# First weight chunk in two transfers, aligned weight rows, and six warming matmuls on a prologue constant, in a cross-attention kernel on one core

## What is computed

```
q = x @ Wq + bq;  k = ctx @ Wk + bk;  v = ctx @ Wv + bv
w = softmax(q @ k.T / sqrt(512), axis = queries)
y = w @ v + x
out = (y - mean(y)) * rsqrt(var(y) + eps) * gamma + beta
```

## Time and profile before

| | us |
|---|---|
| median of 3 runs | 142.45 |
| lowest, highest | 141.98, 142.91 |
| the profiled execution, its own time | 142.72 |
| span of the profiled execution | 141.0 |
| TensorE matmuls busy in the span | 134.5 |
| VectorE, ScalarE, GpSimd busy | 115.1, 79.6, 60.8 |

### The profile page before, as it was taken

One profiled execution on the slowest core, in us unless ns is written; L12 is line 12 of the kernel. 1 busy time (PEld: TensorE's weight loads), 2 busy tenths in 40 slices (PEclk: granted clock), 3 DMA queues, 4 the chain that ended last, 5 costly groups with the idle time before them and its releaser, 6 DMA issues.

```text
span 141.0 us, 2976 instructions
## 1 busy us (share of the span) xinstructions
PE 134.5 (95%) x1046; PEld 130.2 (92%) x1046; DVE 115.1 (82%) x224; ACT 79.6 (56%) x283; POOL 60.8 (43%) x61
## 2 busy tenths in 40 slices
PE   6999999999999999999999999999999999999940
PEld 6899999999998999999999999999999999999940
DVE  0689995996996779999999976878789976797983
ACT  4267098677276925467474829474747546386420
POOL 1000000027304580733849370629475643629791
PEclk9999999999999999999999999999999999999998
DMA  4899999965087495995988799696996965535314
GB/s 152 294 411 417 424 307 394 333 227 204 13 251 274 184 364 153 380 346 188 342 294 297 291 308 382 225 324 211 328 335 227 383 251 203 212 103 196 144 73 150
DMA packets 10814, 37.33 MB, mean 265 GB/s; under 512 B 1200, under 2 KB 1456, under 8 KB 10800
## 3 DMA queue, kind: packets, MB, share of 16 engines
q1 hardware_dynamic: 9424, 34.79, 69.6%
q10 hardware_dynamic: 1376, 2.36, 4.4%
HBM read 33.87 MB, written 3.28 MB: 263 GB/s over the span
## 4 chain that ended last, share of the span: by engine, by line
PE 89%; POOL 5%; issue 2%; ACT 1%; DVE 0%; POOLq 0%; DVEq 0%
PE ps_S L423 29%; PE ps_U L437 26%; PE ps_Y L458 10%; PE ps_U L396 6%; PE ps_Y L396 6%; POOL xT_in L978 3%; PE ps_Y L340 2%; POOL xT_in L966 2%; PE ps_S L344 1%; PE ps_w L446 1%; PE ps_U L503 1%; PE ps_U L350 1%; PE ps_c L411 1%; PE ps_U L355 1%; ACT xT_in L600 1%
## 5 line engine op out<-in xcount | busy, mean ns | idle before, releaser
L582 ACT ACTIVATE expo<-scores,negmax 121x100 f32<-121x100 f32 x96 | 35.0, 365 | 30.9 <-DVE negmax L753 30.9
L423 PE MATMUL ps_S<-G,ctxT_in 128*121 128x100 f32 (+1 forms) x384 | 43.4, 269 | 0.0
L423 PEld LDWEIGHTS ps_S<-G,ctxT_in 128*121 128x121 f32 (+1 forms) x384 | 42.1, 185 | 0.0
L437 PEld LDWEIGHTS ps_U<-prob,ctx_in 121*128 121x128 f32 x336 | 39.4, 192 | 0.9
L437 PE MATMUL ps_U<-prob,ctx_in 121*128 121x100 f32 x336 | 39.6, 274 | 0.0
L955 POOL TENSOR_TENSOR prob<-expo,rinv 121x600 f32<-121x600 f32 x16 | 19.2, 1202 | 30.6 <-DVE rinv L760 30.4
L966 POOL TENSOR_TENSOR xT_in<-x_in,xT_in 128x512 f32<-128x512 f32 (+1 forms) x13 | 17.1, 1315 | 19.8 <-issue 8.9
L749 DVE TENSOR_TENSOR scores<-ps_S,c_rows 121x600 f32<-121x600 f32 x16 | 12.5, 782 | 10.3 <-PE ps_S L423 7.4
L764 DVE TENSOR_REDUCE probsum<-prob 121x100 f32<-121x600 f32 x16 | 19.8, 1237 | 1.0 <-POOL prob L955 0.7
L582 ACT ACTIVATION_READ_ACCUMULATOR expo<-scores,negmax 121x1 f32 x96 | 17.9, 187 | 0.0
L971 POOL TENSOR_TENSOR rstd<-vareps,neg_half 128x1 f32<-128x1 f32 (+1 forms) x13 | 7.1, 549 | 23.3 <-DVE vareps L791 23.1
(11 more groups left out here) (120 smaller groups left out, 185.7 us busy)
## 6 DMA issues: line engine op xcount, KB each, us to landing
ctx_in<-ctx SPq DMA_DIRECT2D x16, 768.0 KB, 4.9
ctxT_in<-ctxT SPq DMA_DIRECT2D x16, 722.0 KB, 5.1
xT_in<-xT SPq DMA_DIRECT2D x8, 400.0 KB, 8.5
x_in<-x SPq DMA_DIRECT2D x12, 256.0 KB, 4.6
out<-xT_in ACTq DMA_DIRECT2D x8, 256.0 KB, 4.0
wqk<-Wqk SPq DMA_DIRECT2D x4, 388.0 KB, 4.6
out<-xT_in SPq DMA_DIRECT2D x3, 256.0 KB, 2.0
wv_in<-Wv SPq DMA_DIRECT2D x1, 512.0 KB, 15.7
```

The source lines that it names most:

```text
L423: last = nc.tensor.matmul(ps_scores(c)[0:rows(c), :], ctxT_in[:, q, l * M + c * MP:l * M + c * MP + rows(c)], G[:, l, bass.ds(b * T, T)], ...
L437: last = nc.tensor.matmul(ps_U[:, q, l * T:(l + 1) * T], ctx_in[0:rows(c), q, c, l * P:(l + 1) * P], prob[0:rows(c), q, c * T:(c + 1) * T] ...
L582: last = nc.scalar.activation(expo[0:MP, q, c * T:(c + 1) * T], scores[0:MP, q, c * T:(c + 1) * T], ACT.Exp, bias=negmax[0:MP, q, c:c + 1] ...
```

## The change

Four things change, all ahead of or at the first weight products.

- The chunk 0 comes in two transfers: first the columns 256 to 770 (the second half of Wq, Wk and the biases, 515 columns), with a semaphore of its own, `first_w_in`; then the columns 0 to 255, which set `w_in[0]`. The other three chunks carry 771 columns instead of 776.
- The halves swap their parts: banks 2 and 3 now get the FP32 product of chunk 0, since their columns come first; banks 0 and 1 get the split products. ScalarE's upper half of chunk 0 is that of columns 0 to 255 and waits for `w_in[0]`; VectorE starts on Wk at `first_w_in` and waits for `w_in[0]` only before the lower half of Wq.
- A row is 784 columns apart in SBUF (3136 bytes, before 3104) and 896 in memory (3584 bytes, before 3104).
- Six warming matmuls instead of seven. They read a constant 1.0 that the program's prologue writes (one column, repeated), stand ahead of the wait for `consts_set`, and so wait for nothing.

```diff
-        WARM = 7
-        wqk = sb("wqk", [P, EC, Wqk.shape[2]])
+        WARM = 6
+        wqk = sb("wqk", [P, EC, E + L + 16])
...
+        first_w_in = sem("first_w_in")
...
         def split_columns(f):
-            return slice(EC // 2 * P, E) if f == 0 else slice(0, E)
+            return slice(0, E // 2) if f == 0 else slice(0, E)
...
         def _(sp):
-            for c in range(EC):
-                sp.dma_start(wqk[:, c, :], Wqk[c]).then_inc(w_in[c], 16)
+            sp.dma_start(wqk[:, 0, E // 2:E + L + 3], Wqk[0, :, E // 2:E + L + 3]).then_inc(first_w_in, 16)
+            sp.dma_start(wqk[:, 0, 0:E // 2], Wqk[0, :, 0:E // 2]).then_inc(w_in[0], 16)
+            for c in range(1, EC):
+                sp.dma_start(wqk[:, c, 0:E + L + 3], Wqk[c, :, 0:E + L + 3]).then_inc(w_in[c], 16)
...
+            unit = nc.const_aps.tensor(1.0, [P, P], F32)
+            for _ in range(WARM):
+                nc.tensor.matmul(ps_Y[:, 0, 0:P], unit, unit, start=True, stop=True)
             pe.wait_ge(consts_set, 1)
-            for _ in range(WARM):
-                nc.tensor.matmul(ps_Y[:, 0, 0:P], ones[:, :], ones[:, :], start=True, stop=True)
-
-            pe.wait_ge(w_in[0], 16)
-            for e in range(EC // 2):
+
+            pe.wait_ge(first_w_in, 16)
+            for e in range(EC // 2, EC):
                 nc.tensor.matmul(banks[e][:, 0:L + 2], wqT[:, 0, e * P:(e + 1) * P], wkT[:, 0, :], start=True, stop=False)
             for f in range(EC):
-                blocks = range(EC // 2, EC) if f == 0 else range(EC)
+                blocks = range(EC // 2) if f == 0 else range(EC)
...
-                dve.wait_ge(w_in[c], 16)
+                dve.wait_ge(first_w_in if c == 0 else w_in[c], 16)
                 nc.vector.tensor_copy(wk_hi[:, c, :], wkT[:, c, :]).then_inc(wkhi_set, 1)
...
+                if c == 0:
+                    dve.wait_ge(w_in[0], 16)
                 dve.wait_ge(wqhi_set, c + 1)
...
-    Wqk = np.zeros((EC, P, E + L + 8), x.dtype)
+    Wqk = np.zeros((EC, P, E + L + P), x.dtype)
```

## The result

The changed kernel takes 142.99 us (median of 22 runs, 142.34 to 143.70), the kernel before 142.44 us (22 runs, 141.88 to 142.91): ratio 1.0042, 95% interval 1.0027 to 1.0056. It is 0.6 us slower, where 0.25 us of gain was forecast. The profiled execution took 143.47 us with a span of 141.7. In the tables further on, a median counts every execution, and a ratio leaves out those more than 1.5% above the kernel's fastest.

What follows compares the result with a forecast made beforehand. TensorE's work, its start and a tail were taken to bound the kernel. An earlier first product, limited by VectorE's chain, gains 0.25 us: 142.72 becomes 142.47, less 0.27 to the median gives 142.2 us, range 141.4 to 143.1.

Steps and rivals of the forecast that it cites:

- the term of the added issue: Head of SP's queue: one transfer more issues chunks 1 to 3 0.45 us later; cost 0 to 0.45, taken as 0.05.
- a sign of being wrong: Weight loads: chunk 2 landing more than 0.2 us later or earlier than 7.31 us would show the prediction wrong.
- The rest of the sum: Last weight products: L365 waits for VectorE's lower half of chunk 3 (9.95), starts at 10.03 instead of 10.27, gain 0.24 us.
- The rival of the added issue: SP's queue: chunks 1 to 3 land the full 0.45 us later, 0.2 lost, 142.6; issue or landing late had chance 0.22.
- The alignment: Weight chunk rows: nothing taken; rival without the dip, chunk 3 1.4 us earlier, 142.1; faster transfers or earlier clock 0.10.
- The rival of the later rise: TensorE's gap before the first product delays the clock's rise to 9.23 us; 1.0 us lost, 143.5; chance 0.10.
- The slack of TensorE: First products of chunk 2: ScalarE's half ready at 7.94 us, TensorE asked at 8.36; slack 0.42, enough for 0.25 gained.

Runs made afterwards that it cites:

- again: The changed kernel as it is, run once more for a second profile; median 142.67 us, ratio 1.0026 to the kernel before.
- whole_first: The changed kernel with chunk 0 in one transfer again; median 142.35 us, ratio 1.0001 to the kernel before.
- align_only: The kernel before with only the new row distances (3136 bytes in SBUF, 3584 in memory) and 771 columns per transfer; median 142.57 us, ratio 1.0016.
- two_queues: The kernel before with chunks 1 and 3 issued from ScalarE's queue, before its table load; median 142.66 us, ratio 1.0030.
- warm_only: The kernel before with only the six warming matmuls on the prologue's constant, ahead of the wait; median 142.47 us, ratio 0.9978.

## Why the prediction was wrong

*What held.* TensorE bounds the kernel, and what happens at L365 passes to the end unchanged: 0.76 us there, 0.7 in the span. The warming starts at 0.81 (0.85 forecast), the first piece lands at 3.52 (3.55), the first product starts at 3.61 (3.60), the second piece lands at 3.87 (3.95), the gap is 0.16 us (0.2).

*The step that failed* is the term of the added issue: "Cost 0 to 0.45; I take 0.05 for the extra packets." Chunks 1 and 2 both came 0.97 us later, outside even the bound, and beyond the 0.2 us for chunk 2 that the prediction itself named as a sign of being wrong. The rest of the sum stands up well. It let L365 wait for VectorE, whose chain hangs on the landing of chunk 2; with 0.97 in place of 0.05 it gives 9.95 + 0.97 + 0.03 = 10.95, and VectorE was through at 10.91 and L369 started at 11.03 (the hand-over, 0.03 in the sum, measured 0.12). In `again` chunk 2 came 0.29 us later than 7.31, VectorE was through at 10.24, L369 started at 10.35.

I reasoned that transfers that land 5.6 us after issue wait for bandwidth, so that their order of arrival depends on bytes alone. But part of that delay was the slow stretch, which I had seen in the earlier trace rows, had weighed only as a matter of alignment, and had otherwise taken as fixed in time. It follows the transfers at the head of the queue: before, it fell on chunk 2; with the split it falls on chunk 1, and chunk 2 comes no earlier for it. Removing the split (`whole_first`) gives the time back; a third piece doubles the loss. What makes the stretch stays open.

*The rival of the added issue* named the right edit and the right sign, 142.6, with 0.2 us of loss instead of 0.6: it priced the issue (0.45 us) and not the stretch. The measured median, 142.99, lies in the range that I gave (up to 143.1) by luck: that end was there for the spread between runs and a late clock.

*The alignment.* I took nothing, and `align_only` shows nothing beyond 1.0016 [0.9997, 1.0034]. The slow stretch is also in it (chunk 2 1.86 us behind chunk 1). By the rule on the start of a row from the Trainium skill, DMA: Bandwidth & Descriptors, How a descriptor splits into AXI transactions, chunk 3 would have come an estimated 0.14 us earlier; no run here shows it.

*The clock.* The rival of the later rise is real, but not in this kernel. Its price was 1.0 us; with a gap of 0.5 to 0.6 us 2 to 7 of some 12 executions per kernel lose 0.8 us or more, up to 1.9. The 0.16 us of the changed kernel don't set it off in any of its 34 executions.

Without such a gap the rise moves by itself. In two executions of the changed kernel it came near 6.9 us (the profile after: the pair of L363 takes 0.55 at 6.14, the one at 6.96 takes 0.31) and near 4.2 (`again`). That agrees with what the Trainium skill says in TensorE: Matmul & The Clock Gate, Part 1, that the watch runs freely.

For the kernel before this also sorts the times. Of its 151 executions beside the experiments, the 67 with a mean granted clock of 0.988 to 0.993 have a median of 142.02 us, the 61 with 0.995 to 0.997 one of 142.70; the profiled one, 0.996, had its rise at 6.75. It is tempting to read the first group as the early rises, and `two_queues` (0.990, full clock by 5.1 us) fits. But the mean doesn't tell the rise from kernel to kernel: `warm_only` has 0.989 with the rise at 9.2, and the changed kernel has 0.994 with 6.9 and 0.999 with 4.2. So how much the split costs at an early and at a late rise can't be read from these groups. Over them the changed kernel's 34 executions have 142.78 (19 executions) and 143.03 (7); that it loses more where TensorE is early is likely from `again`, with its wait of 0.9 us, and not shown.

*The second error* is what the one profile stood for. It had chunk 2 at 7.31, so that VectorE's chain ended at 9.95 and an earlier TensorE could gain little. In the six other profiles with all on SP's queue and chunks 0 to 2 whole, chunk 2 was there at 6.3 to 7.0, and VectorE through at 9.1 to 9.6. The slack of TensorE was no firmer: 0.42 us, where the clock's rise moved by 2.7 us between two executions of one kernel, which is worth half of that in TensorE's time.

## What to carry to other kernels

A transfer added at the head of a queue cost more here than its bytes or its issue: look for the stretch in which the engines move less than elsewhere, find which transfer it falls on, and ask which one it falls on after the change. Before counting on slack at the start of a kernel, look at several executions: here the clock's rise moved by more than 2 us between them. Warming must reach to the first product: one warming matmul too few cost up to 1.9 us in part of the executions, and no version saved anything.

## What the runs showed of the hardware

With all transfers on one queue, the third landed 1.1 to 2.5 us behind the second where it was a whole chunk (ten profiles), and 1.0 and 1.8 us behind where it carried 128 kB; at the lowest microsecond between 3 and 7 us the engines moved 135 to 363 GB/s (13 profiles). With whole chunks on a second queue from 0.8 or 1.1 us on they moved 376 to 419 GB/s from 3 to 6 us (six profiles). Why is open. A gap of 0.5 to 0.6 us in TensorE's first 4 us came with a rise of the clock near 9.2 us in two profiles, of 143.9 and 143.8 us, and by 6.3 in a third, of 142.5 us. And the clock's rise came near 6.9 and near 4.2 us in two executions of one and the same kernel.
